# The first tile's query stacks move into the projections, and the MLP's first weights and three of its W1 products into the attention's tail

## The reference

```python
xn = _layernorm(x, axis=-1)
x = x + _L0_attn_ref(xn, ...) + _L0_ffn_ref(xn, ...)
```

```python
weights = (x @ router_w)[..., 0] + router_b[0]
topv, topi = jax.lax.top_k(weights, k)
sel_idx = jnp.sort(topi[:, :kc], axis=1)                 # kc = k - 1
hn = rmsnorm(x_sel, ln1)
q, kk, v = rope(heads(hn @ wq), pos_sel), rope(heads(hn @ wk), pos_sel), heads(hn @ wv)
sc = jnp.einsum('bhqd,bhkd->bhqk', q, kk) / sqrt(hd) + m_sel[:, None]
o = einsum(softmax(sc), v) @ wo
x1 = x_sel + o
x2 = x1 + gelu(rmsnorm(x1, ln2) @ w1) @ w2               # w1: 512 x 2048, w2: 2048 x 512
out = zeros.at[sel_idx].set(x2 * w_sel) + x * (1 - sel_mask)
```

## Time and profile before

| what | us |
|---|---|
| median of 3 runs | 2056.69 (2056.41 to 2061.67) |
| the profiled execution | 2064.03 |
| its span, first to last instruction | 2062.3 |
| PE busy | 1875.6 (91%) |
| DVE busy | 1431.0 (69%) |
| ACT busy | 876.0 (42%) |
| POOL busy | 153.1 (7%) |

### The profile page before, as it was taken

How to read it: one execution, slowest core, us unless ns; L and a number is a source line. 1 busy time by engine, 2 the same in 40 slices (tenths; PEclk the granted TensorE clock), 3 DMA queues, 4 the chain that set the end, 5 groups by cost and what they waited for, 6 DMA issues and landing times. The chain is left out here.

```text
span 2062.3 us, 72400 instructions
## 1 busy us (share of the span) xinstructions
PE 1875.6 (91%) x32380; PEld 1579.8 (77%) x32380; DVE 1431.0 (69%) x3531; ACT 876.0 (42%) x1504; POOL 153.1 (7%) x187
## 2 busy tenths in 40 slices
PE   6999999999999999999999998249899999877998
PEld 5888888888888888888888786237766666657897
DVE  6777677677777777777777675577478787866222
ACT  4343343334434334334334333214477777754110
POOL 1000000000000000000000000041100000000000
PEclk9999999999999999999999998559999999998999
DMA  4112111111211211211111110215500000005100
GB/s 128 34 34 60 39 34 54 39 39 34 59 39 34 60 39 34 59 39 34 55 44 34 54 34 24 82 55 168 181 17 12 12 12 15 9 2 181 34 11 21
DMA packets 61060, 100.34 MB, mean 49 GB/s; under 512 B 4608, under 2 KB 25104, under 8 KB 60752
## 3 DMA queue, kind: packets, MB, share of 16 engines
q1 hardware_dynamic: 54976, 76.56, 12.2%
q0 software_dynamic: 5776, 19.15, 3.0%
HBM read 51.13 MB, written 27.26 MB: 38 GB/s over the span
## 5 line engine op out<-in xcount | busy, mean ns | idle before, releaser
L331 POOL TENSOR_TENSOR As<-T 128x512 f32<-128x512 f32 x64 | 82.7, 1291 | 1201.1 <-DVE T L610 1201.1
L1900 DVE CUSTOM_DVE_ANT_0 Sm<-Sp,mc 128x1023 f32<-128x1023 f32 x128 | 155.5, 1216 | 15.9 <-PE Sp L1941 8.0
L1806 ACT ACTIVATE Sm<-Sm,least 128x1023 f32<-128x1023 f32 x128 | 146.8, 1147 | 14.9 <-DVE least L1900 13.6
L386 ACT ACTIVATE Pq<-Pq 128x1024 f32<-128x1024 f32 x64 | 68.0, 1062 | 147.7 <-DVE Pq L579 147.7
L1941 PE MATMUL Sp<-KS,QS 128*128 128x512 f32 x256 | 94.6, 452 | 35.8 <-DVE least L1900 34.1
L1852 DVE COPY PTs<-Tp 128x512 f32<-128x512 f32 x128 | 88.1, 688 | 38.8 <-PE Tp L1953 38.4
L366 ACT ACTIVATE QT<-proj 128x512 f32<-128x512 f32 x64 | 38.1, 595 | 178.1 <-PE proj L773 178.1
L349 ACT ACTIVATE DV<-proj 128x512 f32<-128x512 f32 x64 | 38.2, 597 | 177.2 <-PE proj L783 177.2
L2155 PE MATMUL hb<-xT,w1m 128*128 128x256 f32 x768 | 100.5, 289 | 9.5 <-DVE w1m L2211 6.8
L2155 PEld LDWEIGHTS hb<-xT,w1m 128*128 128x128 f32 x768 | 99.3, 198 | 12.5 <-issue 7.2
L1779 ACT ACTIVATE PTs<-Tp 128x512 f32<-128x512 f32 x128 | 76.1, 595 | 62.8 <-PE Tp L1949 61.5
(11 more groups left out here) (313 smaller groups left out, 4852.7 us busy)
## 6 DMA issues: line engine op xcount, KB each, us to landing
VS<-DV SPq DMA_DIRECT2D x64, 264.0 KB, 4.0
xin<-in_x SPq DMA_DIRECT2D x32, 512.0 KB, 5.5
out_rows<-outt SPq DMA_DIRECT2D x64, 256.0 KB, 2.0
mask_columns<-x1T SPq DMA_DIRECT2D x16, 512.0 KB
xs<-in_w SPq DMA_DIRECT2D x16, 512.0 KB, 4.9
QT<-in_wqT SPq DMA_DIRECT2D x1, 1024.0 KB, 6.5
KT<-in_wkT SPq DMA_DIRECT2D x1, 1024.0 KB, 9.5
SQT<-in_wvT SPq DMA_DIRECT2D x1, 1024.0 KB, 15.4
```

What stands on the lines that cost most here:

```text
L331: pool.tensor_tensor(As[:, :], T1[:, :], T2[:, :], ALU.add).then_inc(s_as, 1)
L386: act.activation(Pq[:, :, :, :], Pq[:, :, :, :], ACT.Exp).then_inc(s_exp, 1)
L1806: act.activation(Sm[:, h % 4, 0:KC], Sm[:, h % 4, 0:KC], ACT.Exp, bias=least[:, h % 4:h % 4 + 1], scale=-1.0, accum_out=rsum[:, b, h:h + 1 ...
L1900: dve.tensor_tensor_reduce(Sm[:, h % 4, 0:KC], Sp[h % 2][:, 0:KC], mc[:, b, 0:KC], 1.0, 3.0e38, ALU.add, ALU.min, least[:, h % 4:h % 4 + 1])\
```

## The change

It has three parts.

1. **Query stacks of tile 0.** They are made in the last tile (t = LAST = 7) of the projections. `KS` and `QS` now live to the end of the program, and `qst` and `mc` to the attention's end. Since `QS`, `qst` and `mc` exist during the projections, the weights for them lie there until their last use: the key's high part in `qst` and low part in `mc`, the query's high part in `QS`. GpSimd gathers tile 0's mask at the end of the projections' block.
2. **The MLP's first weights.** W1's and W2's parts come in another order of places (`SLOT`), and the first six loads are issued in the attention's block: three when `keep` has freed their places, three more when earlier parts are split. Four parts of W1 and the first group's tokens are split there. W1 lies in `KS`, the tokens in `QS`, the hidden banks in `Sp`. The table for GELU is fetched by one activation of a single column.
3. **Three W1 products** (hidden(0), (1), (2)) stand between the last tile's steps. The MLP's block begins with hidden(3).

```diff
+        KS = sb("KS", [P, H, K], F32R)
+        QS = sb("QS", [P, H, P], F32R)
...
+            high = [as_weight(qst.rearrange("p h u d -> p h (u d)")), as_weight(QS), vhigh]
+            low = [as_weight(mcr), qlow, vlow]
...
                 for hh in range(2):
                     pool.wait_ge(s_mw[hh], 16 * Q)
 
+                pool.wait_ge(s_q, 3 * LAST + 1)
+                pool.indirect_dma_start(mc[:, 0, :], None, cols_dram,
+                                        bass.IndirectOffsetOnAxis(ap=cidx[:, 0:1], axis=0)).then_inc(s_mg[0], 16)
...
+                def query_high():
+
+                    act.wait_ge(s_q, 3 * LAST + 1)
+                    act.wait_ge(s_r, 2)
+                    act.activation(qst[:, :, 0:2, :], stacked(qrow[:, 0, :]), ACT.Copy).then_inc(s_q0h, 1)
+
+                def query_stacks(gs):
+                    for g in gs:
+                        act.wait_ge(s_q, 3 * LAST + 2)
+                        act.wait_ge(s_rt, G * LAST + g + 1)
+                        act.activation(QS[:, 4 * g:4 * g + 4, :],
+                                       bank[4 + g % 2][:, :].rearrange("p (h k) -> p h k", h=4), ACT.Copy)\
+                           .then_inc(s_kt, 1)
...
                     masks(t, 0)
+                    if t == LAST:
+                        query_high()
                     act.wait_ge(s_r, 2 * t + 1)
...
+                    if t == LAST:
+                        query_stacks((0, 1))
                     act.wait_ge(s_q, 3 * t + 3)
                     act.activation(V[:, t, :], bank[3][:, :], ACT.Copy).then_inc(s_vc, 1)
+                    if t == LAST:
+                        query_stacks((2, 3))
                     stacks(t, (0, 1))
...
+                    if t == LAST:
+                        dve.wait_ge(s_q0h, 1)
+                        dve.tensor_tensor(qst[:, :, 2:4, :], stacked(qrow[:, 0, :]), qst[:, :, 0:2, :].bitcast(F32),
+                                          ALU.subtract).then_inc(s_q0l, 1)
                     dve.wait_ge(s_kh, t + 1)
...
                 sp.dma_start(wo[:, :, :], wo_d.rearrange("(c p) n -> p c n", p=P)).then_inc(s_w, 16)
+                for n in range(Up.EARLY):
+                    if n < 3:
+                        sp.wait_ge(s_keep, 2 * n + 2)
+                    up.load(sp, n)
...
-                stack(0)
-                for g in range(G):
-                    take_stack(0, g)
+                act.sem_inc(s_qh, 1)
+                act.sem_inc(s_qs, G)
                 heads(0, 0, before=False)
                 for t in range(1, Q):
                     heads(t, t % 2, after=t < Q - 1)
+                act.wait_ge(s_s, Q * H)
+                up.high(act, 0)
                 take_t(Q - 1, H - 1)
+                up.high_x(act, 0)
                 take_x1(Q - 2)
+                up.high(act, 1)
                 take_o(Q - 1, G - 1)
+                up.high(act, 2)
                 take_on(Q - 1)
+                act.activation(least[:, 0:1], rinv[:, 0:1], ACT.Gelu_apprx_tanh)
+                up.high(act, 3)
                 take_x1(Q - 1)
...
                 weights(Q - 1, 1)
+                up.low(dve, 0)
+                up.low_x(dve, 0)
+                up.low(dve, 1)
                 attention_rows(Q - 1)
+                up.low(dve, 2)
                 for step in range(5):
                     second_norm(Q - 1, step)
+                up.low(dve, 3)
                 keep(Q - 1)
...
                 values(Q - 1, G - 1, 1)
+                pe.wait_ge(s_sm, Q * H + 1)
+                up.hidden(pe, 0)
                 back(Q - 1)
+                up.hidden(pe, 1)
                 again(Q - 1)
                 project(Q - 1)
+                up.hidden(pe, 2)
                 norm_t(Q - 1)
...
+    EARLY = 6
+    SLOTS = 4
+    SLOT = [0, 1, 2, 0, 1, 2, 3, 0, 1, 2, 3, 0, 1, 2, 3, 0]
+    FIRST = [0, 1, 2, 3, 6, 8, 10, 12]
+    SECOND = [4, 5, 7, 9, 11, 13, 14, 15]
...
+    def load(self, sp, n):
+        before = [k for k in range(n) if self.SLOT[k] == self.SLOT[n]]
+        if before:
+            sp.wait_ge(self.s_wl, before[-1] + 1)
+        sp.dma_start(self.place(n), self.source(n)).then_inc(self.s_wd[self.SLOT[n]], 16)
...
-            hidden(0)
-            hidden(1)
+            up.hidden(pe, FIRST)
             for n in range(U * PAIRS):
-                if n + 2 < U * PAIRS:
-                    hidden(n + 2)
+                if FIRST < n + 2 < U * PAIRS:
+                    up.hidden(pe, n + 2)
                 rows(n)
...
             for n in range(U * PAIRS):
-                for e in (2, 3):
-                    if 2 * n + e < 2 * PAIRS:
-                        high(2 * n + e)
+                for w in (2 * n + 2, 2 * n + 3):
+                    if n >= 2 and w < 2 * PAIRS:
+                        up.high(act, w)
...
+                act.activation(gelu[:, n % 2, :], up.hb[n % 4], ACT.Gelu_apprx_tanh).then_inc(up.s_g, 1)
+                if n < 2:
+                    up.high(act, 4 + n)
```

More of the change, by code:

```diff
@@ L1683, in _ @@
                     stacks(t, (2, 3))
+        Sp = [ctx.enter_context(nc.psum_tensor(f"Sp{i}", [P, 1024], F32)) for i in range(2)]
+        up = Up(nc, ctx, KS, QS, xs2, x1T, Sp, w1_d, w2_d)
         with ExitStack() as c2_:
             wo = sb("wo2", [P, G, D], c=c2_)
-            QS = sb("QS", [P, H, P], F32R, c=c2_)
-            qst = sb("qst", [P, H, 4, DK], F32R, c=c2_)
-            mc = sb("mc", [P, 2, K], c=c2_)
             Sm = sb("Sm", [P, 4, K], c=c2_)
@@ L1703, in feed_forward @@
             t1 = sb("t1", [P, 1], c=c2_)
-            Sp = [c2_.enter_context(nc.psum_tensor(f"Sp{i}", [P, 1024], F32)) for i in range(2)]
             Tp = [c2_.enter_context(nc.psum_tensor(f"Tp{i}", [P, 512], F32)) for i in range(2)]
@@ L2038, in heads @@
                             norm_t(t - 1, after)
-                for g in range(G):
-                    stack(0, g, first=True)
+                pe.sem_inc(s_qp, G)
                 score(0, 0)
@@ L2135, in _ @@
         def _(sp):
-            for n in range(2 * PAIRS):
-                if n >= SLOTS:
-                    sp.wait_ge(s_wl, n - SLOTS + 1)
-                sp.dma_start(place(n), sources[n][1]).then_inc(s_wd[n % SLOTS], 16)
+            for n in range(up.EARLY, 2 * PAIRS):
+                up.load(sp, n)
         @block.tensor
         def _(pe):
-            def hidden(n):
-                u, k = n // PAIRS, n % PAIRS
-                if k == 0:
-                    pe.wait_ge(s_xl, u + 1)
-                if u == 0:
-                    pe.wait_ge(s_wl, first(k) + 1)
-                if n >= 4:
-                    pe.wait_ge(s_g, n - 3)
-                for e in range(2):
-                    f = 2 * k + e
-                    for m, (hx, hw) in enumerate(PARTS):
-                        for c in range(G):
-                            ins = pe.matmul(hb[n % 4][:, e * NT:e * NT + NT], w1[hw][:, c, f * P:f * P + P],
-                                            xT[hx][:, c, :], start=m + c == 0, stop=m == 2 and c == G - 1)
-                ins.then_inc(s_h, 1)
             def rows(n):
@@ L2161, in rows @@
                 if u == 0:
[L2162 removed]
+                    pe.wait_ge(up.s_wl, up.SECOND[k] + 1)
                 pe.wait_ge(s_gl, n + 1)
```

204 lines of the change are left out of this document (128 added, 76 removed).

## The result

The changed kernel took 2045.08 us at the median of six runs (2042.58 to 2048.20), the kernel before 2057.24 in its six (2053.14 to 2061.67): ratio 0.9952, 95% interval 0.9938 to 0.9965. By that ratio it is faster by 9.9 us with an interval of 7.2 to 12.8; the two medians are 12.2 us apart, inside this interval. 15.5 were forecast.

The account below looks back on a forecast made before the run. It took chains of waits at the two barriers around attention, then TensorE in the MLP, as the bound. Terms -6.1 and -9.4 sum to -15.5 us, off the median 2056.69: 2041.2 us, range 2036 to 2047.

Parts of the forecast that it names:

- term B: Attention's tail and MLP start: row products begin sooner with four W1 products done instead of three, -9.4 us.
- term A: Attention's start: query stacks moved into the projections bring VectorE's first score reduction sooner, -6.1 us.
- the block opens between 1490.3 and 1491.3: Barrier from projections to attention: the block opens 0.25 to 1.27 us after ScalarE's end at 1490.0.
- So the new late one is the mask: Attention's start: VectorE's first reduction waits for the mask's gather, landing at 1493.0, and no longer for a query.
- still waiting for that write, to about 1488.6: Same barrier in the kernel before: GpSimd's wait for the mask columns' write explains 1.27 us against 0.25 at the second barrier.
- The loads go out under the last tile's heads on an otherwise quiet queue: nothing.: Last attention tile: issuing the loads of weight parts 0 to 2 there costs nothing.
- Rival 1: MLP's second group: the stall at ScalarE's copy of x goes, 19.7 us less in all, 2037.0; chance 0.12.
- Rival 2: Attention's tail: low clock spreads, products 0 and 1 run at the low level, 4.7 us, 2045.9; chance 0.14.
- Rivals 3 and 4: 3: tail gives back the MLP's saving, 2050.7, chance 0.09. 4: low clock into MLP row products, six pairs 2071.8, chance 0.03.

Follow-up runs that it names:

- query_only: The kernel before with only the first part of the change (tile 0's query stacks and mask gather in the projections): ratio 0.9982 to the kernel before.
- wo_late: The changed kernel with TensorE's wait for Wo moved from ahead of tile 0's heads to behind them: ratio 0.9914 to the kernel before.
- loads_late: The changed kernel with the MLP's first weight loads held until the last tile's scores are reduced: 2053.74 us, ratio 0.9962 to the kernel before.
- inc_only: The kernel before plus seven semaphore increments behind VectorE's keep steps, on which nobody waits: last tile 48.70 us; no whole time given.
- again: The changed kernel once more, unedited: 2046.87 us, ratio 0.9921 to the kernel before.
- before_again: The kernel before, unedited, profiled a second time: last tile 46.74 us; no whole time given.
- before_third: The kernel before, unedited, profiled a third time: last tile 46.70 us; no whole time given.
- changed_pair: The changed kernel, unedited, timed beside another kernel on one chip: 2046.91 us, ratio 0.9955 to the kernel before.
- gather_late: The changed kernel with tile 0's mask gather moved back to the start of the attention's block: 2051.00 us, ratio 0.9947 to the kernel before.
- best_again: Repeat of the changed kernel with later Wo wait, loads held by the reductions' count, W1 product 3 halved, out's gathers later: last tile 46.70 us.

## Why the prediction was off

The direction was right, and so was term B with its mechanism. 5.6 of the 15.5 us forecast did not come (by the ratio), and three steps failed: in term A the gather was taken to hold nothing but VectorE, and TensorE's wait for Wo was not followed; in the last tile the cost was put at nothing.

- **Term A: 2.7 us measured (query_only: the same), 6.1 forecast.** ScalarE ended 15.56 us after the last KEY projection's start, 2.28 later than before; forecast 2.4. Two things failed. First, "the block opens between 1490.3 and 1491.3", that is at most 1.27 us after ScalarE: it was 2.84, since the gather holds the barrier. The mask was there at the first reduction, and the barrier was late in its stead. The step took the gather as a thing that lands on its own, with only VectorE waiting. That makes 1.4 us: the first reduction came 4.68 us sooner and not 6.1. Second, the forecast ended at the first reduction and did not follow TensorE to the wait for Wo, which stands behind two scores in the code that it quotes. Removing the query stacks uncovered it: tile 0 took 1.9 us more, of which some 1.3 are the wait and the rest the clock (wo_late). "So the new late one is the mask" was wrong; the new late ones are the barrier and then Wo.
- The reading that GpSimd, "still waiting for that write, to about 1488.6", held the barrier in before had the engine right and the cause wrong. Its waits for the write were over by 1485.85, and from 1485.97 to 1488.64 it was in its DRAIN, 2.67 us long with nothing under way and the same in six profiles of this code. So the 1.27 us at the barrier are not the receipt of the mask's write, as the prediction read them; they are GpSimd's DRAIN, which ended 1.00 us behind ScalarE's. Why that takes 2.67 us stays open.
- **Term B: 9.3 us, 9.4 forecast.** The last reduction to the row products took 38.3 us on the mean of six profiles with the old tail and 31.8 in the three of the changed kernel, with a product of 2.87 more done (30.8 to 31.8 in all eight with its tail, mean 31.5: then B is 9.7). That the size is so near is in part luck: the old tail spread from 36.7 to 40.3 us with the length of the low level at the MLP's start (10 to 17 us), and between the first two profiles B is 8.8. In the tail each link came as written: the transposes of OTs +3.16 (forecast 3.1), of On +4.97 (5.1), the last +4.92 (5.1), the opening +5.6 (5.8), VectorE ending the block. Only product 3 was taken too short: 5.46 for 4.7, at a granted clock of 0.50 throughout; the prediction's own 218 ns a matmul would have given 5.2:

```profile
1860.30:1865.50 5.20, 5.20 (x24) 5.20 (x25) 4.55 (x7) 4.15 (x6) 0.00 (x0) 0.50 0.78 269
```

- **"The loads go out under the last tile's heads on an otherwise quiet queue: nothing."** Of the loads this holds (loads_late). But the edit that times them put an instruction into VectorE's stream, which is the bound of that tile, and the sentence counted only the DMAs. It cost 2.5 us: 0.8 for the increments and 1.7 for two low stretches. The increments alone, in the kernel before, made 2.0 of it with one stretch (inc_only); the second stretch, 0.5 us, is not traced to a cause, and query_only shows that one can come without any increment.
- **Rival 1** (the stall goes) describes the first profile and is not the change's doing: again has the stall, before_again and before_third do not. **Rival 2** put the low clock into products 0 and 1, which ran at 3.11 and 3.12 us. It came instead in the last tile and in product 3. **Rivals 3 and 4** did not come.
- The sum by these terms, -2.7 - 9.3 + 2.5 = -9.5 us, is what the first timing (-9.9, interval -12.8 to -7.2) and changed_pair show; again's -16 is more than its profile's distances account for.

## What to carry over

When a stretch of work is taken out, follow each engine past the first instruction that comes sooner, to the next wait that the stretch had covered; here that wait was two scores away. Count work that is in flight at a block's end as part of the block: a GpSimd gather issued just ahead of the barrier moved the barrier, though nobody inside waited for it. Count what a new wait needs on the side that signals it, and hang it on a count that the busy engine raises anyway.

## What the runs showed of the hardware

- A barrier behind a gather of 512 KB under way opened 5.9 to 6.3 us after the gather's issue, in thirteen profiles: GpSimd's DRAIN ended 1.39 or 1.40 us after the landing in each. Without a gather under way this DRAIN took 2.67 us, in seven profiles, and in gather_late, where that was over first, the block opened 0.26 us after ScalarE.
- A semaphore increment of its own on VectorE between two dependent operations makes 0.12 us (0.33 against 0.21).
- TensorE's clock fell to 1.2 GHz in the middle of attention behind 6.0 us in which TensorE was busy for 2.30 (after) and 5.5 in which it was busy for 2.44 (inc_only). It stayed up in before_third and best_again, with 2.53 and 2.72 of 6.0. The Trainium skill ("TensorE: Matmul & The Clock Gate", Part 1: The HAM clock gate) says that the clock falls when the array has been idle, and tells of a kernel with short idle times between its groups of matmuls in which it went down and up. These traces show the second: the clock fell in the midst of steady work with many short waits. The window of best_again:

```profile
1799.00:1805.00 6.00, 2.72 (x32) 2.05 (x36) 5.71 (x11) 3.08 (x5) 0.00 (x0) 1.00 0.26 87
```

- The same code spread by 4 to 15 us between executions, and the first stage alone by 8 us between two profiles. Steps of 1 to 2 us were read from distances inside a profile; those of the changed kernel repeat to about 0.1 us, while the old tail moves by up to 3.6 us with the length of the low level.
